# A recommender tower on one core: Gram matrices two samples at a time in their own bank pair, and another order of pieces on every engine

## The reference, cut to what matters

```
e = stack([tbl_f[ids[:, f]] for f in range(26)])      # 2048 x 26 x 64, gathered rows
x = LN(dense @ Wd.T)                                  # 2048 x 128
y = LN(e @ Ws.T)                                      # 2048 x 26 x 128, LN over 128
y = LN(einsum('bne,pn->bep', y, Wsi))                 # 2048 x 128 x 32, LN over 32
T = concat([x, y^T])                                  # 2048 x 33 x 128
Z = einsum('bnd,bmd->bnm', T, T)                      # a 33 x 33 Gram matrix per sample
z = LN(Z[lower triangle] @ Wl.T)[:, :384]             # 528 pairs -> 512, LN, mask
h = relu(concat([z, dense]) @ W_top1 + b_top1)        # 512
h = relu(h @ W_top2 + b_top2)                         # 256
out = h @ W_top3                                      # 2048 x 1
```

## Time and profile before

| | |
|---|---|
| median of three runs | 626.21 us (625.28 to 627.51) |
| the profiled execution | 628.74 us, span 626.9 us |
| mean granted TensorE clock | 0.946 of full |
| busy share PE, DVE, POOL, ACT | 83%, 83%, 64%, 47% |
| indirect gathers | 416 |

### The profile page before, as it was taken

One profiled execution on the slowest core, in us unless ns is written; L12 is line 12 of the kernel. 1 busy time (PEld: TensorE's weight loads), 2 busy tenths in 40 slices (PEclk: granted clock), 3 DMA queues, 4 the chain that ended last, 5 costly groups with the idle time before them and its releaser, 6 DMA issues.

```text
span 626.9 us, 17592 instructions
## 1 busy us (share of the span) xinstructions
PE 520.4 (83%) x6955; PEld 394.3 (63%) x6955; DVE 519.8 (83%) x1073; ACT 295.3 (47%) x730; POOL 402.9 (64%) x422
## 2 busy tenths in 40 slices
PE   1462777777899999999998899899998989979886
PEld 1352556545576767676767677676776676747665
DVE  3499689899999999999998979999999898986500
ACT  0410343445465556464636445555555464635422
POOL 6777775767777777777777777777777777200000
PEclk9955887798999999999999899999999999999999
DMA  7311111111111111111111111111111111000000
GB/s 176 109 24 33 27 28 30 28 34 27 35 28 36 28 37 27 37 28 31 34 28 36 29 36 27 37 27 37 28 36 28 29 27 28 14 1 2 2 1 1
DMA packets 22610, 20.22 MB, mean 32 GB/s; under 512 B 12017, under 2 KB 14721, under 8 KB 22529
## 3 DMA queue, kind: packets, MB, share of 16 engines
q0 software_dynamic: 13312, 13.66, 12.1%
q1 hardware_dynamic: 8400, 4.33, 2.7%
q10 hardware_dynamic: 816, 1.11, 0.6%
HBM read 19.07 MB, written 0.01 MB: 30 GB/s over the span
## 4 chain that ended last, share of the span: by engine, by line
PE 37%; DVE 24%; issue 16%; ACT 8%; POOL 8%; DMA 3%; SPq 2%; ACTq 0%; DVEq 0%; POOLq 0%
PE b_l L418 10%; POOL emb L255 8%; PE b_y L342 7%; PE b_l L396 5%; DVE nrm L778 3%; DVE byn L788 3%; DVE V L811 3%; DVE yb L793 3%; DVE var_y L800 3%; PE b_a L321 3%; PE b_z L354 3%; DVE prod L757 2%; DMA emb<-in_tbl,idx 2%; ACT mixed L505 2%; PE b_a L312 2%
## 5 line engine op out<-in xcount | busy, mean ns | idle before, releaser
L255 POOL DMA_INDIRECT emb<-in_tbl,idx x416 | 402.2, 967 | 134.7 <-issue 118.5
L510 ACT ACTIVATE sq<-yb 128x1024 f32<-128x1024 f32 x64 | 67.7, 1059 | 191.1 <-DVE yb L793 187.2
L342 PE MATMUL b_y<-mixed,projw 64*128 64x512 f32 x256 | 74.9, 663 | 23.8 <-ACT mixed L505 23.8
L793 DVE TENSOR_TENSOR yb<-b_y,bias_y 128x1024 f32<-128x1024 f32 x64 | 78.1, 1220 | 19.9 <-PE b_y L342 19.5
L811 DVE TENSOR_TENSOR V<-yb,rstd_y 128x256 f32<-128x256 f32 x256 | 91.9, 422 | 2.2
L800 DVE TENSOR_REDUCE var_y<-sq 128x32 f32<-128x1024 f32 x64 | 77.8, 1215 | 6.9 <-ACT sq L510 5.6
L396 PE MATMUL b_l<-wlt,zt 128*128 128x512 f32 x160 | 72.9, 603 | 0.5 <-ACT zt L561 0.5
L330 PE MATMUL b_mix<-mix,byn 128*128 128x128 f32 x512 | 72.4, 287 | 0.0
L321 PE MATMUL b_a<-gram_w,embt 128*128 128x128 f32 x416 | 66.3, 303 | 6.3 <-ACT embt L494 5.6
L354 PE MATMUL b_z<-V 128*32 128x34 f32 x4096 | 58.2, 200 | 12.5 <-DVE V L811 9.7
L330 PEld LDWEIGHTS b_mix<-mix,byn 128*128 128x128 f32 x512 | 66.4, 203 | 0.2
(11 more groups left out here) (131 smaller groups left out, 681.7 us busy)
## 6 DMA issues: line engine op xcount, KB each, us to landing
emb<-in_tbl,idx POOLq DMA_INDIRECT x416
dense<-in_r_dense_t SPq DMA_DIRECT2D x16, 128.0 KB, 2.3
V<-in_L_rec_Wl ACTq DMA_DIRECT2D x1, 1056.0 KB, 5.2
w<-in_W_top SPq DMA_DIRECT2D x2, 512.0 KB, 7.0
w<-in_W_top SPq DMA_DIRECT2D x1, 768.0 KB, 5.3
out_y<-y_sb SPq DMA_DIRECT2D x16, 0.5 KB
idx<-in_ids SPq DMA_DIRECT2D x1, 195.0 KB, 5.1
wd<-in_L_rec_Wd SPq DMA_DIRECT2D x1, 128.0 KB, 4.1
```

What stands on the lines that cost most here:

```text
L255: pool.indirect_dma_start(out=emb[t % 2][:, f, :], out_offset=None, in_=tables[f], in_offset=bass.IndirectOffsetOnAxis(ap=idx[:, t, f:f + ...
L342: last = nc.tensor.matmul(b_y[:, j2, :], projw[r, :], mixed[c % 2][r, :], start=True, stop=True, tile_position=(64 * j2, 0))
L793: nc.vector.tensor_tensor(yb[c % 2][:, :, :, :].rearrange("e h s p -> e (h s) p"), b_y[:, :, :].rearrange("e h (s p) -> e (h s) p", p=NP), ...
```

## The change

**Gram matrices by pairs.** `V` is laid out for two samples side by side: 68 columns (`PAIRED`), in which x and ones stand at either end and the 64 columns of y between. `gram` takes 16 matmuls of 64 columns by 68 in place of 32 of 32 by 34, two column groups in place of four; the products of one sample with the other are computed and not read. Its result takes two banks (`b_z` is now a pair). To free one, `b_l0` is now the same bank as `b_x`, with waits added to keep its users apart. `copy_zs` takes four instructions, one for each 32 partitions, since the useful columns stand in two different places. `zs` has the sample index outside now, with contiguous writes, and `by_sample` reads it with a stride. The last part of `pair_rows` is a piece of its own (`pair_x`), with two accumulating matmuls. `copy_x` writes `V` in four instructions.

**Layout of `nrm`.** `normalize` now writes contiguously, and `shuffle` reads with a stride of 64 elements.

**Order.** Each engine takes its pieces in another order, and pieces are in other quarters:

| piece | quarter before | quarter now |
|---|---|---|
| dense_transposes, dense_project, dense_back | 2, 2, 4 | 0, 1, 2 |
| normalize, both halves; shuffle | 3, 5; 5 | 2, 4; 4 |
| mix_features, project | 6 + c, 6 + c | 5 + c, 6 + c |
| scale | 7 + c | 6 + c |
| gram | 7 + c | 7 + c |
| by_sample, pair_rows, interact | 12, 12, 13 | 11, 11, 12 |
| interact's norm, interact_back | 14, 15 | 13 and 14, 14 |
| layer1, layer2, layer3 | 18 and 19, 20, 21 | 15, 15, 16 |

QUARTERS falls from 83 to 79. The gathers' wait on `gram_done` has the same count, but is tested at features 0, 7, 13 and 20 of a tile. The core of the diff, without the lists of `if` lines:

```diff
-        nrm = sb("nrm", [P, D, NP])
+        nrm = sb("nrm", [P, NP, D])
...
-        V = [sb(f"V{h}", [P, 2, 4, 4, NQ, GRAM]) for h in range(2)]
-        zs = [sb(f"zs{h}", [P, GRAM, NJ]) for h in range(2)]
+        V = [sb(f"V{h}", [P, 4, 2, 4, 2, PAIRED]) for h in range(2)]
+        zs = [sb(f"zs{h}", [P, NJ, SLOTS]) for h in range(2)]
...
+        b_l0 = b_x
...
                 for j in range(8):
-                    for q in range(NQ):
-                        v = V[t % 2][:, j % 2, c, j // 2, q, :]
-                        last = nc.tensor.matmul(b_z[32 * q:32 * q + 32, GRAM * j:GRAM * (j + 1)], v[:, 0:NP], v, start=True, stop=True)
+                    for q in range(2):
+                        v = V[t % 2][:, c, j % 2, j // 2, q, :]
+                        last = nc.tensor.matmul(b_z[64 * q:64 * q + 64, j // 4, PAIRED * (j % 4):PAIRED * (j % 4 + 1)], v[:, 2:2 + 2 * NP], v,
+                                                start=True, stop=True, tile_position=(0, 64 * q))
...
-                nc.scalar.activation(zs[t % 2][:, :, 8 * c:8 * c + 8].rearrange("p c j -> p j c"),
-                                     b_z[:, 0:8 * GRAM].rearrange("p (j c) -> p j c", c=GRAM), ACT.Copy).then_inc(zs_copied, 1)
+                for q in range(NQ):
+                    r, slot, first = slice(32 * q, 32 * q + 32), 2 * (q % 2), GRAM * (q % 2)
+                    last = nc.scalar.activation(
+                        zs[t % 2][r, 8 * c:8 * c + 8, slot:slot + GRAM].rearrange("p (a j) c -> p a j c", a=2),
+                        b_z[r, :, 0:4 * PAIRED].rearrange("p a (j c) -> p a j c", c=PAIRED)[:, :, :, first:first + GRAM], ACT.Copy)
+                last.then_inc(zs_copied, 1)
...
-                    nc.vector.transpose(byn[t % 2][:, :, d].rearrange("p j d -> p d j"), nrm[:, d, :]).then_inc(byn_ready, 1)
+                nc.vector.transpose(byn[t % 2][:, :, d].rearrange("p j d -> p d j"), nrm[:, :, d].rearrange("p n d -> p d n")).then_inc(byn_ready, 1)
```

More of the change, by code:

```diff
@@ L464, in _ @@
[L464 to L475 removed]
+                if (x := part(h, 1)):
+                    transposes(*x)
@@ new lines, in _ @@
+                if (x := part(h, 6)):
+                    project(*x)
+                if (t := tile(h, 1)) is not None:
+                    dense_project(t)
+                if h == 10:
+                    prepare_wlt(4)
+                if (x := part(h, 1)):
+                    norms(*x)
+                if (t := tile(h, 16)) is not None:
+                    layer3(t)
+                if (t := tile(h, 14)) is not None:
+                    interact_back(t)
+                if h == 6:
+                    prepare_wlt(0)
@@ L477, in _ @@
+                if (t := tile(h, 2)) is not None:
+                    dense_back(t)
         @block.scalar
@@ new lines, in _ @@
+                if (t := tile(h, 13)) is not None:
+                    deviation_o(t)
+                if (t := tile(h, 2)) is not None:
+                    scale_x(t)
+                if (x := part(h, 8)):
+                    copy_zs(*x)
+                if (t := tile(h, 14)) is not None:
+                    copy_z(t)
+                if (t := tile(h, 15)) is not None:
+                    relu1(t, 0)
+                if (x := part(h, 6)):
+                    square_y(*x)
+                if (x := half(h, 2)):
+                    deviation_n(*x)
@@ L639, in _ @@
+                if (x := part(h, 6)):
+                    deviation_y(*x)
+                if (t := tile(h, 15)) is not None:
+                    relu2(t)
         @block.vector
@@ L851, in _ @@
[L851 to L860 removed]
+                if (x := part(h, 6)):
+                    add_bias(*x)
+                if h == 5:
+                    fold_sums()
+                if (t := tile(h, 11)) is not None:
+                    by_sample(t, 0)
@@ new lines, in _ @@
+                if h == 4:
+                    fold(1)
+                    prepare_mlp()
+                if h == 7:
+                    prepare_wlt(0)
+                if (t := tile(h, 11)) is not None:
+                    by_sample(t, 1)
+                if h == 8:
+                    prepare_wlt(1)
+                if (x := part(h, 1)):
+                    norms(*x)
+                if h == 5:
+                    prepare_gain()
+                if (x := half(h, 2)):
+                    bound_n(*x)
```

329 lines of the change are left out of this document (155 added, 174 removed).

## The result

The changed kernel takes 637.68 us (median of 4, 637.22 to 637.83), the kernel before 626.62 on the same chip: a ratio of 1.0177, interval 1.0157 to 1.0197. It is 11 us slower, 1.8%, with an interval that lies wholly above 1, where the prediction said 11 us faster.

The account below looks back on a forecast made before the run. The prediction took POOL's gathers, 32.9 us a tile, as the bound, with gains only from waits and tail: -4 + 1 - 8.1 - 3.2 + 3 = -11.3 on a 626.9 us span, so 615 us, range 606 to 637.

Parts of the forecast that it names:

- The bound: Steady state: POOL's 416 gathers of 1.267 us set the pace, 32.9 us a tile, with PE and DVE close behind.
- The start, -4: Program start: first Gram part 4 to 5 us earlier, POOL's 6.5 us of waits shrink; 4 us gained.
- the new waits of the shared bank: Waits added for the shared bank: each names a piece ahead in the same quarter or the one before; cost nothing.
- The steady state, +1: Engines' longest round of four quarters: 32.6 us summed, 32.3 to 33.3 against POOL's 32.9; 1 us lost.
- Rival C: Engines' round a little longer, 33.5 to 34.2, by handoffs and ACT's slower copies: 622 to 631 us, chance 0.16.
- `shuffle` and `by_sample`, "I take nothing": DVE transposes that now read and write with strides: the penalties overlap, so nothing is added.
- rival A: DVE's transposes: both strides cost, 2.3 us more work a round, round 34.9, total 640 us; chance 0.18.
- `gram`, side by side: PE's Gram part: two 64-column groups run in parallel, 1.0 us a part, about unchanged; one after the other 2.0.
- The later start of the drain, +3: After the last gather: PE begins the last batch 6.4 us behind it, not 3.4; 3 us lost.
- the drain, -3.2: From the last norms to the last Gram part: 46.4 us for 49.6, so 3.2 gained.
- The tail, -8.1: From the last Gram part to the end of the span: 27.4 us for 35.5, so 8.1 gained.
- B: PE's Gram parts: the two groups don't run side by side, round 34.8, total 639 us; chance 0.10.

Follow-up runs that it names:

- x6: Changed kernel with both old layouts (single-sample Gram matrices, `nrm` as before), still with one bank for the folded weights: 626.64 us, ratio 0.9996 to the kernel before.
- x5: x6 with the fourth piece of the folded weights a quarter later and the fifth behind the Gram part: 619.36 us, ratio 0.9891 to the kernel before.
- e3: Changed kernel with ACT's copy of the mix moved ahead of `deviation_n` and the relu of layer 1: 637.32 us.
- e2: Changed kernel with the old layout of `nrm` (strided writes, plain read in the shuffle): 630.28 us.
- e1: Changed kernel with the old Gram form (single samples, old `V`, `zs`, `zb`, single `b_z`); new order, shared bank and `nrm` kept: 630.41 us.
- e4: Changed kernel with the fourth piece of the folded weights, `prepare_wlt(3)`, at quarter 9 in place of 8: 635.10 us.
- x1: Same kernel as x6, run while the kernel before took 800 to 809 us; engines' round 41.4 us, total time not given in the text.

## Why the prediction was wrong, step by step

**The bound.** "The program runs at POOL's pace" was right for the kernel before, and the whole sum was then made at POOL. Once the engines' round is the longer one, what counts is how late PE is. In the prediction's own terms the sum came out so (span, us):

```
                                        forecast  measured
start: POOL's waits, to the fourth tile   -4        +4.1
rounds behind it, at POOL                 +1        +3.2
PE later behind the last gather           +3        +7.3
last batch to last Gram part              -3.2      +0.2
behind the last Gram part                 -8.1      -6.9
```

POOL's last gather of the fourth tile ends at 145.54 for 141.40, that of the last at 545.74 for 538.42. The second and third line together are what PE's rounds lost: the 8.6 from the fourth tile on, and 1.9 that it had fallen behind POOL by then. The largest miss is the start. POOL's gathers are also a little longer here (976 ns for 967, 0.23 us a tile); why isn't shown.

**The start, -4: wrong in sign, +6.1 at the fourth tile.** The first Gram part did come sooner (74.83 for 76.83, not the 4 to 5 forecast). The step that failed is "the new waits of the shared bank I cost at nothing": I looked at the waits of the steady state and not at `prepare_wlt`, whose two banks the change makes one. PE stands 10.2 us for them. In the order alone the fourth tile is 4.2 us later than before, and with two of the pieces moved 1.1 earlier, which is 5.3 us at that tile and 7.3 us of time (x6 to x5, on two chips; by the ratios to the kernel before it is 6.6). The other 1.9 of the 6.1 come with the two layouts (155.67 for x6's 153.81). No run gives the pieces their second bank back, so that the merged bank and not the new order alone makes the stall is read from the waits and the code, not tested. POOL's largest wait, 6.04 at 112.45, is new with it.

**The steady state, +1: the path wrong in q2, and +8.6 at PE.** The round is 33.4, not 32.6. DVE's q0 came out (10.9 against 10.95, though the terms listed for it add up to 10.7: a shuffle of 4.2 for 3.7 made up for shorter writes and for a wait that isn't there). PE from the `project` of the q3 through that of the q0 takes 2.89 + 9.33 + 1.11 = 13.3 where I had 12.2 + 1.5 = 13.7. What failed is the rest, "DVE in q1 up to its sum of squares 3.7, two short ACT steps 0.9, PE in q2 from `norms` to `dense_back` 3.4", and as a path, not in its sizes. The timeline of the changed kernel there:

```profile
437.94 1.21 DVE L837 TENSOR_REDUCE var_y<-sq 128x32 f32<-128x1024 f32 x1
...
440.12 0.94 PE L320 MATMUL b_a<-gram_w,embt 128*128 128x128 f32 x6
...
443.48 0.49 PE L311 MATMUL b_a<-ident,emb 128*128 128x128 f32 x3
444.63 1.13 PE L341 MATMUL b_y<-mixed,projw 64*128 64x512 f32 x4 [0.66 <-ACT mixed L519]
```

From 435.52 to 443.48 it takes 7.96, the 8.0 forecast. But then come the transposes of the q3 (0.49), which no term names, and PE stands 0.66 for the copy of the mix: the path that ends last stays on DVE through q1 and into q2 and comes back over ACT, 5.76 + 3.35 = 9.1. Cutting that link alone gives nothing, since the norms' copy comes almost as late (e3).

Then "between 32.3 and 33.3 against 32.9" was taken as a small loss. But the kernel before made its rounds at 32.68 on PE, since it was catching up (it was 8.2 behind the gathers at the fourth tile and 3.4 at the last), so each round lost 0.72. Rival C comes nearest: its round of 33.5 to 34.2 begins just above what was measured, and handoffs are in its reason, ACT's copies of `zs` are not in the chain. Its 622 to 631 missed the time because it kept the -4 of the start, the +3 and the drain.

**`shuffle` and `by_sample`, "I take nothing".** Wrong, and rival A was a true mechanism at a third of its price: a second stride adds 0.28 us to a 1.93 us shuffle. With `by_sample` that is 0.92 a tile, 0.17 of it for the wider third transpose. That is past the 0.7 from which the rival was to decide, but only the shuffle's 0.57 lies in the round, and undoing the layout took 0.40 off it (e2). The Trainium skill ("SBUF — State Buffer", the note on cachelines) was weighed there. It gives no size; the second stride costs well below the 0.7 of the first, so the first one's price taken twice overstates it.

**`gram`, side by side.** Right: 1.17 us for a part, where one after the other would be 2.0. The Trainium skill's rule on tiles that work in parallel ("TensorEngine Tiling (Array Packing)", Key Properties) fits: the time of L353 is that of two groups side by side. The pair Gram form still costs 0.55 a round beside the new `nrm` (33.40 against e1's 32.85), on PE in the q3: 0.16 in the Gram part and 0.38 in the x part of the pair rows (0.92 for 0.54 in e1).

**The later start of the drain, +3; the drain, -3.2.** PE comes 10.7 behind the last gather, 7.3 more than before, not 3; the six quarters to the last Gram part take 49.8, 0.2 more. A part of that, and of the tail, is the clock: PE stands 1.62, 2.04 and 0.67 us near the end, the granted clock is 0.62 in 600 to 607 (1.00 in 585 to 592 before), and the last Gram part takes 2.08 for 1.17 and the first half of layer 1 behind it 3.4 for 2.2. That is some 2 us which no term of the forecast has. With both layouts undone it is 48.2 (x6), with the start mended too 46.5 (x5), about what I had forecast for the whole change. Why the start matters there I didn't test.

**The tail, -8.1: -6.9**, right within 1.2. It stays between 29 and 32 in all versions of the new order. In the best one, x5, the span is 9.3 shorter than before: 2.9 at PE's last batch, 3.0 in the drain, 3.4 in the tail.

**The range.** 606 to 637 was too narrow by the prediction's own chances: rivals A and B, 0.28 together, were priced at 640 and 639, above its upper end, though no more than 0.2 was to lie outside.

**How the losses add.** The order alone has a round of 32.1 us while it catches up (x6: 153.81 to 185.89), when PE waits for no gather. POOL in the same run takes 33.0 a tile (its last gathers end at 144.52 in the fourth tile and 540.26 in the last), so the slack is 0.9. With either layout the round is 32.85 or 33.00, just inside it, and with both 33.40. In time each layout alone costs 3.6 to 3.8 us over x6, since PE no longer catches up, and both together 11.0. This is only a reading of four runs on more than one chip. The parts don't quite add (32.1 + 0.75 + 0.9 = 33.75 for 33.40). The order by itself (x6) comes to the time of the kernel before: its last batch is 4.1 us later, and its drain 1.4 and its tail 5.0 shorter.

## What to carry to other kernels

When one engine sets the pace by a narrow margin, work out the round of the others link by link, follow it once around in the trace, and look for a second link of nearly the same length: an edit to one of them alone gains nothing (e3, where the second lay 0.2 us behind). When two banks become one, look at every place that used both, the code that runs once at the start too. A stall there was paid in full at the end, both with the engines setting the pace (e4) and with POOL setting it (x5 against x6). Two changes that each fit into the slack may not fit together: price them as a sum against the slack, not one by one.

## What the runs showed of the hardware

* A 32 x 32-block transpose of 1024 elements per partition that writes with a stride takes 1.93 us; reading with a stride as well makes it 2.21 (changed kernel and e1, against e2 and x6). One of 512 goes from 1.06 to 1.14.
* Plain writes of `nrm` show 286 ns for 384, but six of them together take 1.30 us for 1.50, so of 98 ns a write 33 were gained.
* 32 matmul records of 68 columns in two 64-column groups take 1.17 us, 64 records of 34 columns in four groups 0.76 to 1.00. The last part, behind stands of PE, takes 2.08 (changed kernel, granted clock 0.62 in 600 to 607) and 1.14 (e1, 0.50 in 596 to 600).
* After standing for 3.4 us PE did the same four projection records in 2.08 us that take 1.13 in the steady state, at a granted clock of 0.50 in 90 to 95 us against 1.00 in 200 to 500.
* For a stretch of time, on three chips, PE's stream had gaps of up to 1.3 us within the Gram parts (x1) for which the trace has no cause. The kernel before was 28 to 29% slower, while the durations on DVE and POOL were unchanged (`add_bias` 1218 ns for 1214, a gather 967 for 967). What it was stays open.
